# A pairwise field projection on one core: x gathered for two tiles at a time, in rows of 16,384 bytes

## What is computed

```python
# r_x: (2048, 32, 64) float32, L0_rec_W: (496, 64, 64) float32
PAIRS = combinations(range(32), 2)        # 496 pairs (i, j), i < j
xi = x[:, pi, :]
xj = x[:, pj, :]
proj = einsum('bpd,pod->bpo', xi, W)
return proj * xj                          # (2048, 496, 64)
```

## Time and profile before

| | |
|---|---|
| time, median of 3 runs | 669.47 us (668.73 to 669.98) |
| the profiled execution's own time | 670.16 us |
| its span, first to last instruction | 668.4 us |
| PE, DVE, ACT, POOL busy | 86%, 61%, 35%, 63% of the span |
| moved by DMA | 285.15 MB, mean 427 GB/s |
| granted TensorE clock, mean | 0.958 |

### The profile page before, as it was taken

One profiled execution on the slowest core, in us unless ns is written; L12 is line 12 of the kernel. 1 busy time (PEld: TensorE's weight loads), 2 busy tenths in 40 slices (PEclk: granted clock), 3 DMA queues, 4 the chain that ended last, 5 costly groups with the idle time before them and its releaser, 6 DMA issues.

```text
span 668.4 us, 7464 instructions
## 1 busy us (share of the span) xinstructions
PE 577.2 (86%) x2704; PEld 340.8 (51%) x2704; DVE 410.9 (61%) x528; ACT 232.1 (35%) x301; POOL 419.1 (63%) x256
## 2 busy tenths in 40 slices
PE   5998989989898998979979898898989979799930
PEld 4565555545455554645545455465555645456510
DVE  0776666856566665665856566465666756567630
ACT  2334334343333334333243333233334243433400
POOL 0866848585765866757585774666748575656720
PEclk9999999999999998998999999798999999999975
DMA  8999999999999999999999999999999999999997
GB/s 347 436 437 427 435 422 433 439 429 429 437 429 430 432 433 426 443 433 428 428 431 433 426 432 436 433 427 432 424 428 436 434 429 423 444 423 437 440 424 321
DMA packets 11257, 285.15 MB, mean 427 GB/s; under 512 B 1776, under 2 KB 1904, under 8 KB 2672
## 3 DMA queue, kind: packets, MB, share of 16 engines
q1 hardware_dynamic: 8496, 270.27, 94.1%
q0 software_dynamic: 2464, 14.68, 5.2%
q10 hardware_dynamic: 288, 0.08, 0.1%
HBM read 25.56 MB, written 260.05 MB: 427 GB/s over the span
## 4 chain that ended last, share of the span: by engine, by line
DMA 55%; PE 22%; POOL 7%; DVE 6%; issue 3%; ACT 2%; SPq 0%; DVEq 0%; ACTq 0%; POOLq 0%
DMA out_dram<-staged 37%; PE proj L378 19%; DMA x_in<-x_dram,rows_sb 18%; DVE staged L427 6%; POOL staged L301 6%; PE proj L356 3%; ACT staged L343 2%; DMA ident_sb<-ident_dram 1%; PE proj L400 1%; POOL x_in L283 0%; POOL x_in L274 0%; ACT x_t L328 0%; SPq L248 0%; DVEq L424 0%; ACT x_sb L321 0%
## 5 line engine op out<-in xcount | busy, mean ns | idle before, releaser
L378 PE MATMUL proj<-w_sb,x_t 64*128 64x512 f32 (+7 forms) x2432 | 540.1, 542 | 43.0 <-ACT staged L343 26.8
L427 DVE TENSOR_TENSOR staged<-proj,x_sb 128x1024 f32<-128x1024 f32 (+7 forms) x528 | 410.9, 826 | 231.5 <-PE proj L378 199.9
L301 POOL TENSOR_TENSOR staged<-staged,x_sb 128x1024 f32<-128x1024 f32 (+4 forms) x224 | 390.5, 1756 | 215.3 <-ACT staged L343 211.1
L378 PEld LDWEIGHTS proj<-w_sb,x_t 64*128 64x128 f32 x2432 | 307.9, 190 | 260.0 <-issue 123.8
L343 ACT ACTIVATE staged<-proj 128x1024 f32<-128x1024 f32 (+4 forms) x224 | 171.3, 786 | 323.4 <-PE proj L378 267.0
L321 ACT ACTIVATE x_sb<-x_in 128x2048 f32<-128x2048 f32 x14 | 26.7, 1910 | 68.5 <-DMA x_in<-x_dram,rows_sb 68.5
L356 PE MATMUL proj<-ident_sb,x_sb 128*128 128x128 f32 x256 | 37.1, 292 | 14.3 <-DVE staged L427 14.3
L356 PEld LDWEIGHTS proj<-ident_sb,x_sb 128*128 128x128 f32 x256 | 29.6, 148 | 33.2 <-DVE staged L427 27.3
L328 ACT ACTIVATE x_t<-proj 128x512 f32<-128x512 f32 (+1 forms) x62 | 34.7, 609 | 13.1 <-PE proj L356 13.1
L283 POOL DMA_INDIRECT x_in<-x_dram,rows_sb x14 | 14.5, 1036 | 3.0 <-issue 1.3
L274 POOL DMA_INDIRECT x_in<-x_dram,rows_sb x14 | 13.9, 991 | 2.5 <-issue 2.5
## 6 DMA issues: line engine op xcount, KB each, us to landing
out_dram<-staged SPq DMA_DIRECT2D x16, 5504.0 KB, 24.4
out_dram<-staged SPq DMA_DIRECT2D x15, 5472.0 KB, 24.9
out_dram<-staged SPq DMA_DIRECT2D x16, 4896.0 KB, 25.3
out_dram<-staged SPq DMA_DIRECT2D x1, 3520.0 KB, 16.6
w_sb<-w_dram SPq DMA_DIRECT2D x1, 2944.0 KB, 21.3
out_dram<-staged SPq DMA_DIRECT2D x1, 1952.0 KB, 12.8
w_sb<-w_dram SPq DMA_DIRECT2D x1, 1664.0 KB, 12.1
w_sb<-w_dram SPq DMA_DIRECT2D x1, 1408.0 KB, 14.9
```

What stands on the lines that cost most here:

```text
L301: last = nc.gpsimd.tensor_tensor(product, product, x_sb[tile.parity][:, j * dim:(j + n) * dim], ALU.mult)
L378: last = nc.tensor.matmul(proj[b][h][:, at:at + width], x_t[half, turned_at(i, fields), :], w_sb[half, col:col + width], start=True, stop= ...
L427: last = nc.vector.tensor_tensor(staged_part(item, i, j, n), proj[b][h][:, at:at + n * dim], x_sb[tile.parity][:, j * dim:(j + n) * dim], ...
```

## The change

Rows are dealt to tiles in another way: tiles 2k and 2k+1 hold the even and the odd ones of rows 256k to 256k+255. With x seen as 1024 rows of 16,384 bytes, one such row holds a row for the even tile and one for the odd. One gather (7 in all, and 7 small ones for partitions 16 to 18) brings both into `x_pair`; the even tile works on its left half in place, and ScalarE copies the right half to `x_odd`, once for each pair. Stores of a tile now go to every second row of the output (`tile.parity * out_row`), with the same row pieces. The gather for the next pair is issued in the odd tile: its small DMA before step 1, the large one before step 4. turn_low stands before step 19, and in odd tiles waits for the gather itself. SBUF needs the same space.

```diff
-TURN_LOW_BEFORE = 16
+TURN_LOW_BEFORE = 19
-APART_BEFORE = 6
-GATHER_BEFORE = 13
+APART_BEFORE = 1
+GATHER_BEFORE = 4
-APART = range(15, 20)
+APART = range(16, 19)
...
-        x_in = sb("x_in", [P, fields * dim])
-        x_sb = [sb(f"x_sb{h}", [P, fields * dim]) for h in range(2)]
+        x_pair = sb("x_pair", [P, 2 * row])
+        x_odd = sb("x_odd", [P, row])
+        x_of = [x_pair[:, 0:row], x_odd[:]]
...
+                    to = tile.parity * out_row + first * dim
+                    sp.dma_start(out[bass.ds(tile.half * P, P), to:to + n * dim],
...
-            def load_apart(number):
-                if number > 2:
-                    pool.wait_ge(x_moved, number - 2)
+            def load_apart(tile):
+                _, b, use = list(items(Tile(tile.number - 1, 0, tile.half)))[-1]
+                pool.wait_ge(emptied[b][1], use + 1)
+                pool.wait_ge(pool_scaled[group_of[pool_steps[-1]]], tile.number)
+                if tile.half > 0:
+                    pool.wait_ge(x_moved, tile.half)
...
+            def load_x(tile):
+                pool.wait_ge(x_apart_loaded, 16 * (tile.half + 1))
...
-                    if item == MOVE_BEFORE and not tile.first and not tile.last:
+                    if item == MOVE_BEFORE and not tile.first and not tile.parity:
                         move_x(tile)
...
-                nc.scalar.activation(x_sb[1 - tile.parity][:], x_in[:], ACT.Copy).then_inc(x_moved, 1)
+                nc.scalar.activation(x_odd[:], x_pair[:, row:], ACT.Copy).then_inc(x_moved, 1)
...
+                        elif item == "turn_low" and tile.parity:
+                            pe.wait_ge(x_loaded, 16 * (tile.half + 1))
                         elif item == "turn_low":
-                            pe.wait_ge(x_moved, tile.number)
+                            pe.wait_ge(x_moved, tile.half)
```

53 lines of the change are left out of this document (26 added, 27 removed).

## The result

The changed kernel takes 673.01 us (median of 6 runs, 672.3 to 674.34), the kernel before 669.59 us in 6 runs beside it. The ratio is 1.0048, with a 95% interval of 1.0035 to 1.0061: slower by 0.5%, some 3.4 us. The forecast was 668.7 us, and its range ended at 671.6. The profiled execution took 673.09 us, with a span of 671.3.

The account below looks back on a forecast made before the run. The prediction took the DMA engines' packets, laid end to end, as the bound: -0.55 us for packets and some -0.3 for spread rows, -0.8 in all, from 669.47 to 668.7 us; range of 8 in 10, 666.4 to 671.6.

Parts of the forecast that it names:

- The bound: Kernel before: time is the 16 DMA engines' packets laid end to end, plus the start and the uneven end.
- How much compute may be late: Stores land 24.4 us after issue and take 13.1, so some 11 us of waiting covers late compute.
- TensorE: At turn_low before step 19 of odd tiles: waits 2 us (0 to 5) for the gather, price 0 under the cover.
- GpSimd: Odd tile, before the large gather: stands still 2 to 4 us for the small DMA's landing, price 0 under the cover.
- Rival D: Store queue runs dry in odd tiles because GpSimd's wait holds back the first store: 675.7 us, chance 0.12.
- Rivals C and E: C (0.22): end lag from packets stretched during gathers halves, 667.3; E (0.02): 14 DMAs' fixed 2.0 us on the path, 641.5.
- Packets: Gathers: 896 double rows at 611 ns replace 1792 at 309; with fewer completions, -0.55 us for every engine.
- ScalarE: Seven copies of 1.910 us and the waits for gathers before them go; price 0, as they lie under the stores' queue.
- Dealing and pitch: Stores to rows twice as far apart, in the same pieces: 0, bounds -1 and +1 us.
- Balance: Small DMAs relieve one slow engine of 12.8 us, before perhaps 17.3; it gets 4.5 back, bounds 0 and 8.8.
- rival B: The slow engine, relieved of 12.8 us instead of 17.3, ends last: +0.7 us, 670.2, chance 0.22.
- The end: End of the run: the last packets' spread is 2.5 to 5 us.

Follow-up runs that it names:

- dealt_only: Kernel before with only even and odd rows dealt to tiles and the stores' pitch doubled, x gathered as before: 670.41 us, ratio 1.0012.
- old_small_late: Kernel before with the small DMA issued before step 12 in place of 6, so GpSimd waits for it in every tile: 692.74 us, ratio 1.0334.
- pair_8k_both: Changed kernel with each pair gathered as two gathers of 8,192-byte rows at the same places, TensorE waiting for both: 688.88 us, ratio 1.0264.
- pair_8k_first: pair_8k_both with TensorE waiting for the even tile's half alone: 671.56 us, ratio 1.0027.
- pair_roomy: Changed kernel with two pair buffers, no move by ScalarE, gathers issued a tile earlier, W 2048 columns short in SBUF: 674.57 us, ratio 1.0068.
- first_5rows: pair_8k_first with partitions 15 to 19 in the small DMAs in place of 16 to 18: 670.71 us, ratio 1.0016.
- roomy_8k_each: pair_roomy with gathers of 8,192-byte rows, the even half gathered in the even tile, the odd half in the odd: 672.01 us, ratio 1.004.

## Why the prediction was wrong, step by step

**The bound** was right for the kernel before: the 16 engines' packets end to end, with store landings on the chain. For the changed kernel it holds only as an account (packets, idle time and uneven end add up to the +2.9 us). By my own sign, a time outside 666 to 672 meant that the DMA engines were not the bound or that the new pitch cost something. dealt_only leaves the pitch 1.5 us at most. The chain of the changed kernel shows the first: it runs through TensorE and the gathers' landings, and the packets got longer because compute was late.

**"How much compute may be late" is the step that failed.** I took 24.4 - 13.1 = 11 us as cover. The time from issue to landing is no measure of lead. Read from the packets, the lead is the time from a store's issue to its first packet: 7.0 us in the median of the kernel before, but 3.3 at the lowest, and some 0.9 of it passes even where a DMA engine has run out of store packets (twelve stores of old_small_late lie at 0.85 to 1.3). So where it is lowest it is some 2.5 us and not 11. The lead is also a stock and not a fresh allowance for each tile: what one wait takes must be won back before the next. And the even tile gives little time to win it back where its own start waits for the gather and TensorE's clock is at its lower level behind that wait. old_small_late measured it in the kernel of before: a wait of 7.4 us a tile, under the 11, cost 22.9 us.

**TensorE**: I gave its wait 2 us (0 to 5) and the price 0. It was 5.5 us a pair, 38.5 in all. The landing after the issue was as forecast, 21.5 us on average against 23.8, but TensorE asked 16.0 us after the issue and not 21.5, since GpSimd issues it after its own wait while TensorE runs on. pair_8k_both and pair_8k_first show by a single wait that it is what uses the lead up. That the wait also brought the lower clock I had not thought of; how much of the loss is the clock's stays open. **GpSimd**: 2 to 4 us forecast, 4.7 measured. pair_8k_first shows that such a wait is nearly free, as I had said, while TensorE's isn't there; but old_small_late shows that it isn't free at four times the sum (105 us in 14 tiles against 25).

**Rival D** (the store queue runs dry in odd tiles, 675.7) is what happened, with another first cause: I hung it on GpSimd's wait alone and asked where 11 us would be used up. It struck in three odd tiles of seven, and over all seven its size was 2.9 / 7, about 0.4 us each and not 1. What I did not know is that a dry store queue costs twice. Idle engines are 11.3 engine-us, the gather's packets without store packets beside them 64.7.

**Rivals C and E**: the end did become evener, by 0.8 us of the 1.4 that C counted on; no run tells whether the smaller number of gathers did it. Of E's 28 us nothing was seen.

**Packets**: the price of a double row was right to the ns, 611, and with it the 0.45 us that fewer descriptors save; for the 0.1 of fewer completions there is no run of its own. That its packets or its neighbours would be stretched was in no row of before, where gathers' excess was 1.2 engine-us. In pair_roomy that alone, with next to no wait for a gather, costs 2.3 us: so by this estimate the change would have lost even with the cover that I gave it. This is a second error of the packets' step, independent of the first.

**ScalarE**: price 0, and 7 copies (13.3 us) with no idle time before them, as said. Its row in the page of the changed kernel:

```profile
L334 ACT ACTIVATE x_odd<-x_pair 128x2048 f32<-128x2048 f32 x7 | 13.3, 1902 | 0.0
```

**Dealing and pitch**: within -1 to +1; dealt_only says +0.1 to +1.5 us. **Balance**: the slow engine is real, and worth 12.3 us without small DMAs. In the changed kernel it isn't last, all engines are late. With the waits gone, five rows in place of three give 0.85 us at most likely (first_5rows), where I had 0.7 for rival B. **The end**: the last engine ended 2.1 us after the median one, less than the 2.5 to 5 I gave.

What stays open: pair_8k_first and roomy_8k_each lie 1.7 and 2.2 us above the kernel before though their packets take 0.4 and 0.9 us more; dealt_only's 0.5 to 0.8 us is part of it at best. How much of the changed kernel's loss comes of the wait itself and how much of the lower clock behind it is open too. And why an engine's packets are stretched by 16,384-byte rows beside them: I know that it follows the rows' size and not their place, no more.

## What to carry to other kernels

Where DMA is the bound, a wait on a compute engine is free only out of the lead that compute has over the stores. Read the lead at its lowest, from a store's issue to its first packet (3.3 us before, 0.9 after), not from issue to landing, and count it as a stock that all waits of a cycle draw on. The waits for store landings (86 us in all before, 21 after) are a hint, but can be large and the queue run dry all the same (old_small_late). Look for loops: if the chain that ended last goes through every gather and no store, an engine waits for a transfer and its lateness delays the issue of the next one. Then splitting one wait can be worth more than all the bytes. Look at TensorE's granted clock behind each long wait as well. Fewer, larger DMA rows need not be cheaper: price them by the packets beside them too.

## What the runs showed of the hardware

A gather's packet of 16,384 bytes takes 611 ns when it alternates with store packets, but 969 to 1778 ns in the windows above, where next to no store packets were under way; in old_small_late packets of 8,192 bytes did the same (159 engine-us of excess). The Trainium skill ("DMA: Bandwidth & Descriptors", Queues, rings and completion order) says that an engine takes turns between the queues that have work for it; the row of 389.4 to 393.5 us, 74 packets of q0 and 2 empty ones of q1, is the case in which there is no turn to take. That the packets get longer in it is what the rows add; why, they don't tell. The same page (Latency and other measured facts) gives HBM's access latency as 0.2 us on average and 2 us at high load; no run here shows whether that is the time seen.

Four stores of the changed kernel have their first packet 0.9 to 1.5 us after their issue, on the DMA engine that is first free. In tile 9 it is 4.4 us, where a gather had been issued 3.7 us earlier.

TensorE's granted clock stood at 0.50 for 82 us before the changed kernel's last matmuls, in eight stretches. The six long ones, of 6.8 to 17.1 us, each began while TensorE waited for a gather (waits of 3.6 to 7.6 us).

Rows of 16,384 bytes stretch the store packets beside them from 1.62 to as much as 2.33 us; over a run they cost 44 engine-us more in pair_roomy than rows of 8,192 bytes in roomy_8k_each (83.6 against 39.2).

One DMA engine is slower than the other fifteen: without small DMAs it ended 8.5 us after the median of them in the old kernel, and 8.3 in the changed one.
